# Load order and router weights in a one-core language-model tower: seven loads held behind the first gathers, one expert weight ahead of the first tile rows, router weights made during the expert tiles

## The chip, the core and the metric

The kernel runs on one core of a Trainium2 chip. The metric is the device time of one execution in microseconds (us). The kernel before was timed three times: median 885.13 us, from 883.92 to 888.87.

## What is computed

Token ids (32 sequences of 96) go through three residual blocks; everything is in 32-bit floating point.

```python
x = emb[tokens] * sqrt(128) + positional
q, k, v = x @ Wq + bq, x @ Wk + bk, x @ Wv + bv
scores = einsum('d,bijd->bij', attn_scale, tanh(q[:, :, None, :] + k[:, None, :, :]))
x = layer_norm(x + softmax(scores) @ v @ Wo + bo)
h = layer_norm(x + relu(x @ W1 + bf1) @ W2 + bf2)
h = h + causal_attention_8_heads(layernorm(h))
...
n = layernorm_affine(layernorm(h))
vals, idx = top_2(softmax(n @ Wr @ codebook.T / 0.7))
w = vals / sum(vals)
moe = sum over the two chosen of 64 experts of w * (silu(n @ W1[e] + b1[e]) @ W2[e] + b2[e])
hmoe = moe + 0.25 * (silu(n @ Ws1 + bs1) @ Ws2 + bs2)
return h + hmoe + silu(layernorm_affine(hmoe) @ Wf1 + fbf1) @ Wf2 + fbf2
```

Since the two weights of a token sum to one, they follow from the gap between its second and first logit: with g = exp(gap / 0.7) they are 1 / (1 + g) and g / (1 + g).

## The kernel before

The program is written engine by engine. Each engine runs its own list in order, and semaphores tie them together. SP issues nearly all loads, GpSimd (POOL) the indirect ones.

**Start.** SP sends the ids, then five small loads (semaphore `ld_a`), then seven loads under `ld_b` (wvT, wo, and the five of `ROWS`, each one row of 512 bytes repeated over 128 partitions). VectorE makes indices from the ids, and GpSimd gathers the embedding rows of the first two pairs of sequences with four indirect loads (semaphores `emb0` and `emb1`, 16 * G for a pair, line 491). SP waits for `emb0` and then sends 15 `late` loads, of which the first four are 512 KB each. With `emb0` there, VectorE's `x_rows(0)` (line 904) starts the work. `setup` on TensorE (lines 1343 and 1344), between the first two blocks of scores, and on VectorE (lines 913 to 915) wait for all of `ld_b`. `products` (line 1366) waits for all of `late`.

**Pairs.** 16 pairs of sequences go through a software pipeline (`in_turns`), in which each engine has a fixed order of stages of up to six pairs. Beside it SP fills a region of DRAM with zeros (`rows_dram`, 64 experts with room for every token) and stores x. At the end of a pair each token's row is scattered twice into `rows_dram`, to the next free place of each of its two experts.

**Expert tiles.** From the counts VectorE builds a table of tiles of 128 rows (`ttab`): some 84 tiles, of which 52 (`FIXED`) are written out and the rest run in loops of 8. For each tile SP loads the weights of its expert (`load_expert`, 578 KB, 16 slots) and the rows are loaded (`load_rows`, 64.5 KB, 8 buffers; the first 8 by SP, the others by ScalarE). TensorE transposes rows (line 1635), multiplies with the first weight (1642), ScalarE applies SiLU (771), TensorE multiplies with the second (1653), VectorE adds the bias (1216), and GpSimd stores the results with an indirect store (`store_rows`, 590). The order in which SP starts is set by `ROWS_FIRST`:

```python
for t in range(ROWS_FIRST):
    load_expert(t)
sp.wait_ge(s["scat"], 16 * TOPK * B)
load_rows(sp, 0)
for t in range(1, ROWS_AHEAD):
    load_rows(sp, t)
    load_expert(t + ROWS_FIRST - 1)
```

After weight 23 (slot reuse waits for the tile 16 before) SP loads the residual back from DRAM (`x_back`, 3072 rows of 512 bytes) and then goes on with weight 24. VectorE waits in `hb_affine(t)` (line 1210) until the store of tile t - 8 has landed. The gaps of the logits are brought into token order by TensorE at tile 9 (`relay`) and copied by VectorE at tile 11 (`take_relaid`, semaphore `gaps_t`).

**Last stage.** The shared expert is computed for 12 blocks of 256 tokens: eight of them before the tiles, the last four (`SHARED_LATE`) behind them (TensorE 1525 and 1535, ScalarE 706, VectorE's `shared_rows`, 1092). SP loads the results back block by block (`er0` and on). ScalarE makes exp(gap / 0.7) with an exchange of its table before and after (lines 792 to 794); VectorE makes the two weights (1256 to 1260) and then, for each block, `mixture` (1267 to 1286, with a power on GpSimd, 603, for the square root) and `output` (1295); TensorE has `f_turn` (1689), `last1` (1697) and `last2` (1708).

## Time and profile before

| | us |
|---|---|
| median of three runs | 885.13 |
| lowest and highest | 883.92, 888.87 |
| the profiled execution | 880.4 |
| its span in the profile | 878.6 |

| engine | busy us (share of the span) |
|---|---|
| TensorE (PE) | 781.5 (89%) |
| TensorE weight loads (PEld) | 603.4 (69%) |
| VectorE (DVE) | 656.6 (75%) |
| ScalarE (ACT) | 657.5 (75%) |
| GpSimd (POOL) | 323.0 (37%) |

The profile page gives busy times, the DMA queues and the chain that ended last; the trace behind it gives each instruction's start and duration, what ended the idle time before it, the granted clock of TensorE (1.00 is 2.4 GHz, 0.50 is 1.2 GHz) and the busy share of the 16 DMA engines in any stretch. All times below count from the start of the span. An `SPq` row is a DMA issue by SP; of a row that stands for several instructions (x4), the second number is their time together.

### The profile page before, as it was taken

Reading aid. Unit: us, or ns where it says so; the run is one execution under the profiler, and the core shown is the slowest. Engines: PE = TensorE matmul, PEld = TensorE weight load, DVE = VectorE, ACT = ScalarE, POOL = GpSimd, SP = SyncE. Lnnn points to the kernel's source line nnn. Section 1 sums busy time; section 2 is a strip of 40 time slices with the busy share of each in tenths; the row PEclk is TensorE's granted clock in tenths of the full one; section 3 lists DMA queues with packets and bytes.
Section 4 is the critical chain, followed back from the end, with each engine's and each line's share of the span. In section 5 each row is a group of like instructions: output and inputs, shape, how many; then the busy total and the mean of one; then the engine's idle time right before and its main releaser. Section 6 shows DMA issues by size and latency. Waiting matters only on the chain. (4 is left out here: it accounts for less than half of the span.)

```text
span 878.6 us, 22649 instructions
## 1 busy us (share of the span) xinstructions
PE 781.5 (89%) x7286; PEld 603.4 (69%) x7286; DVE 656.6 (75%) x2161; ACT 657.5 (75%) x1502; POOL 323.0 (37%) x397
## 2 busy tenths in 40 slices
PE   1777998988998989989899999898889999999798
PEld 0454675665665766756667666665679999999687
DVE  3999889989999999999999999453523435443675
ACT  2787989989898898988998999675335655655454
POOL 3110322325334343353343432444414545545121
PEclk9999999999999999999999999997989999999799
DMA  7239889889889889989898898894199999994411
GB/s 149 65 83 210 190 188 210 194 189 212 186 196 210 187 198 207 197 189 206 181 211 181 182 209 178 195 208 97 45 321 397 377 395 403 307 362 161 150 30 37
DMA packets 82305, 177.77 MB, mean 202 GB/s; under 512 B 8244, under 2 KB 35339, under 8 KB 82240
## 3 DMA queue, kind: packets, MB, share of 16 engines
q1 hardware_dynamic: 65536, 164.01, 74.8%
q0 software_dynamic: 5760, 7.92, 2.7%
q10 hardware_dynamic: 10944, 5.02, 2.1%
q8 instruction: 35, 0.57, 0.3%
q14 instruction: 30, 0.25, 0.1%
HBM read 65.93 MB, written 113.34 MB: 204 GB/s over the span
## 5 line engine op out<-in xcount | busy, mean ns | idle before, releaser
L890 DVE TENSOR_TENSOR arena<-qT,b_qk 128x2304 f32<-128x2304 f32 x128 | 323.8, 2543 | 1.6 <-DVE v_bias L915 0.3
L616 ACT ACTIVATE arena<-arena 128x2304 f32<-128x2304 f32 x128 | 271.6, 2123 | 35.7 <-DVE arena L890 34.4
L1322 PE MATMUL b_s<-arena,apad 128*32 128x192 f32 x3072 | 159.2, 343 | 27.1 <-ACT p L625 18.5
L771 ACT ACTIVATE act_h<-big,arena 128x128 f32<-128x128 f32 x336 | 95.8, 368 | 74.6 <-PE big L1642 70.2
L1322 PEld LDWEIGHTS b_s<-arena,apad 128*32 128x32 f32 x3072 | 89.9, 113 | 83.9 <-issue 41.5
L542 POOL TENSOR_TENSOR kept<-kept,rs 96x384 f32<-96x384 f32 x64 | 52.6, 823 | 208.2 <-DVE rs L1025 208.0
L590 POOL DMA_INDIRECT eo_dram<-gT,toff x84 | 82.5, 982 | 97.2 <-issue 67.1
L668 ACT ACTIVATE kept<-kept,mx 96x96 f32<-96x96 f32 x256 | 92.3, 365 | 13.3 <-DVE mx L1018 13.3
L1642 PE MATMUL big<-hbT,arena 128*128 128x128 f32 x672 | 91.1, 279 | 2.4 <-DVE hbT L1205 1.4
L1642 PEld LDWEIGHTS big<-hbT,arena 128*128 128x128 f32 x672 | 83.4, 195 | 3.2 <-issue 2.3
L1205 DVE TENSOR_SCALAR hbT<-b_t,cols 128x128 f32<-128x128 f32 x84 | 34.4, 409 | 65.4 <-PE b_t L1635 65.4
L1489 PEld LDWEIGHTS b_o<-vv,prT 96*96 96x96 f32 x512 | 61.0, 165 | 13.2 <-issue 10.8
L1489 PE MATMUL b_o<-vv,prT 96*96 96x128 f32 x512 | 68.6, 278 | 0.0
L560 POOL DMA_INDIRECT rows_dram<-rows_now,slot_now x64 | 61.1, 955 | 17.8 <-issue 15.6
L1449 PE MATMUL big<-kept,xaT 128*96 128x512 f32 x128 | 66.1, 600 | 0.0
L1018 DVE CUSTOM_DVE_ANT_0 kept<-big,mask 96x96 f32<-96x96 f32 x256 | 49.2, 249 | 18.9 <-PE big L1464 15.7
L1464 PE MATMUL big<-gT,xaT 128*96 128x384 f32 x128 | 54.0, 505 | 2.5 <-DVE mx L1018 2.5
L668 ACT ACTIVATION_READ_ACCUMULATOR kept<-kept,mx 96x1 f32 x256 | 49.1, 192 | 0.0
L1439 PE MATMUL big<-xaT,kept 128*128 128x192 f32 x256 | 46.7, 326 | 0.4 <-ACT xaT L653 0.4
L662 ACT ACTIVATE vv<-big 96x512 f32<-96x512 f32 x64 | 38.0, 594 | 10.1 <-PE big L1449 9.8
L1653 PE MATMUL b_s<-arena,act_h 128*128 128x128 f32 x336 | 45.1, 278 | 0.0
L1653 PE MATMUL b_qk<-arena,act_h 128*128 128x128 f32 x336 | 44.5, 275 | 0.3 <-ACT act_h L771 0.3
(208 smaller groups left out, 1413.8 us busy)
## 6 DMA issues: line engine op xcount, KB each, us to landing
rows_dram<-act_h SPq DMA_DIRECT2D x32, 3096.0 KB
arena<-in_wpack SPq DMA_DIRECT2D x84, 578.0 KB
prT<-rows_dram ACTq DMA_DIRECT2D x76, 64.5 KB
arena<-eo_dram SPq DMA_DIRECT2D x4, 512.0 KB, 7.2
x_dram<-res SPq DMA_DIRECT2D x16, 96.0 KB
out<-of SPq DMA_DIRECT2D x12, 128.0 KB, 1.8
eo_dram<-gT,toff POOLq DMA_INDIRECT x84
rows_dram<-rows_now,slot_now POOLq DMA_INDIRECT x64
```

Source lines behind the costliest of these rows:

```text
L560: pool.indirect_dma_start(rows_dram, bass.IndirectOffsetOnAxis(ap=slot_now[:, j:j + 1].bitcast(U32), axis=0), rows_now[:, j, :], None, bou ...
L590: pool.indirect_dma_start(eo_dram, bass.IndirectOffsetOnAxis(ap=toff[:, r:r + 1].bitcast(U32), axis=0), eo[r], None, bounds_check=TOPK * T ...
L616: act.activation(v, v, ACT.Tanh).then_inc(s["tanh"], 1)
L668: last = act.activation(pr[:, j, :], pr[:, j, :], ACT.Exp, bias=mx2[:, j:j + 1], scale=-1.0, accum_out=es2[:, j:j + 1])
L771: last = act.activation(act_h[:, i, c * TILE:(c + 1) * TILE], big[i][:, c * TILE:(c + 1) * TILE], ACT.Silu, bias=wslot[:, slot, 2 * DFF + ...
L890: dve.tensor_tensor(ring[c % TRING].rearrange("p (x m n) -> p x m n", m=CQ, n=N), qv.unsqueeze(3).to_broadcast([D, SPLIT * QG, CQ, N]), kv ...
L1322: last = pe.matmul(b_s[32 * a:32 * a + 32, 0:SPLIT * N], apad[:, 31 - line:63 - line], t[:, :, a, m, :], start=(line == 0), stop=(line == ...
L1449: pe.matmul(BANK_V[k][0:N, :], xaT[:, g * N:(g + 1) * N], vo[:, (k % 2) * 512:(k % 2 + 1) * 512], start=True, stop=True).then_inc(s["hv"], 1)
L1464: pe.matmul(BANK_S[k][0:N, 0:4 * N], xaT[:, g * N:(g + 1) * N], gT[:, h:h + 4, g * N:(g + 1) * N], start=True, stop=True).then_inc(s["s2"], 1)
L1489: last = pe.matmul(p_o[:, g, :], prT[:, g * H + h, :], vv[:, g, h * D:(h + 1) * D], start=False, stop=(k == 3 and h == H - 1))
L1642: last = pe.matmul(big[of_ring(t, 2)][:, c * TILE:(c + 1) * TILE], wslot[:, slot, c * D:(c + 1) * D], hbT[:, of_ring(t, 2), :], start=True ...
L1653: last = pe.matmul([b_s, b_qk][of_ring(t, 2)][:, 0:D], act_h[:, of_ring(t, 2), c * TILE:(c + 1) * TILE], wslot[:, slot, DFF + c * D:DFF + ...
```

## The change

Three things change.

1. SP's wait for `emb0` stands ahead of the seven `ld_b` loads, which now follow it, with the 15 late ones behind.
2. `ROWS_FIRST` is 1, not 3: SP sends one weight, rows 0, rows 1, weight 1, rows 2, weight 2 and so on. From the 18th of these loads on the order is the same.
3. exp(gap / 0.7) is made on GpSimd as a power of the constant exp(1 / 0.7) (`weigh`, after the store of tile 12), and the two weights on VectorE in tiles 21, 22 and 23. ScalarE's Exp and its two exchanges of tables at the end are gone. Two of the four late shared blocks (`shared_rows` 10 and 11) move behind the residual sum of `mixture(0)`, and TensorE's wait for them from before `f_turn(0)` into `last2(0)`.

```diff
--- before.py
+++ after.py
@@ -43,7 +43,7 @@
 NO_ID = 8192
 SHARED_LATE = 4
 RESIDUALS = 3
-ROWS_FIRST = 3
+ROWS_FIRST = 1
 QG = 4
 SPLIT = 2
 QM = N // (QG * SPLIT)
@@ -174,6 +174,7 @@
         gaps = sb("gaps", [N, PAIRS * G])
         gaps_t = sb("gaps_t", [128, NT])
         gap_e = sb("gap_e", [128, NT])
+        base_e = sb("base_e", [128, NT])
         wts = sb("wts", [128, NT, TOPK])
         rows_now = sb("rows_now", [N, G * TOPK, DC])
         slot_now = sb("slot_now", [N, G * TOPK], I32)
@@ -372,12 +373,12 @@
             load(wqk[:, 1, :], io["L0_tok_Wk"], s["ld_a"])
             load(cols[:, :], io["cols"], s["ld_a"])
 
+            sp.wait_ge(s["emb0"], 16 * G)
             load(wvT[:, :], io["tok_WvT"], s["ld_b"])
             load(wo[:, :], io["L0_tok_Wo"], s["ld_b"])
             for n in ROWS:
                 load(rows[n][:, :], io["row_" + n].partition_broadcast(128), s["ld_b"])
 
-            sp.wait_ge(s["emb0"], 16 * G)
             for i, n in enumerate(["Wq", "Wk", "Wv", "WoT"]):
                 load(raw[:, i, :].rearrange("p (h d) -> p h d", h=H),
                      io["attn_" + n].rearrange("(h k) d -> k h d", h=H), s["late"])
@@ -498,6 +499,7 @@
                     b = p * G + g
                     gather_rows(res[0:N, p, g, :], eidx[:, b:b + 1], s[f"emb{p}"])
             pool.memset(halves[:, 2 * G:], 0.5)
+            pool.memset(base_e[:, :], float(np.exp(1.0 / TEMP)))
             pool.memset(fhalf[:, :], -0.5).then_inc(s["pool_c"], 1)
             pool.memset(cum, 0.0).then_inc(s["pool_c"], 1)
             pool.iota(choice[:, :], [[TOPK * N, B], [1, TOPK]], base=-NO_ID, channel_multiplier=TOPK,
@@ -591,8 +593,14 @@
                     eo_dram, bass.IndirectOffsetOnAxis(ap=toff[:, r:r + 1].bitcast(U32), axis=0),
                     eo[r], None, bounds_check=TOPK * T - 1, oob_is_err=False).then_inc(s_st[r], 16)
 
+            def weigh():
+                pool.wait_ge(s["gaps_t"], 1)
+                pool.tensor_tensor(gap_e[:, :], base_e[:, :], gaps_t[:, :], ALU.pow).then_inc(s["gap_e"], 1)
+
             for t in range(FIXED):
                 store_rows(t)
+                if t == RELAY + 3:
+                    weigh()
             blocks = blocks_less(pool, 0)
             with pool.Fori(0, blocks) as v:
                 for r in range(BLOCK):
@@ -787,11 +795,6 @@
             for j in range(NB - SHARED_LATE, NB):
                 silu_shared(j)
 
-
-            act.wait_ge(s["gaps_t"], 1)
-            act.preload_act_table(ACT.Exp)
-            act.activation(gap_e[:, :], gaps_t[:, :], ACT.Exp, scale=1.0 / TEMP).then_inc(s["gap_e"], 1)
-            act.preload_act_table(ACT.Silu)
 
             def silu_last(j):
                 for c in range(FC):
@@ -1222,6 +1225,17 @@
                                 b_y[:, NT * TOPK:NT * (TOPK + 1)].rearrange("p (a m) -> p a m", a=TILES3))\
                     .then_inc(s["gaps_t"], 1)
 
+            def weights(i):
+                if i == 0:
+                    dve.wait_ge(s["gap_e"], 1)
+                    ch.link(dve.tensor_scalar(gaps_t[:, :], gap_e[:, :], 1.0, None, ALU.add))
+                elif i == 1:
+                    ch.wait()
+                    ch.link(dve.reciprocal(wts[:, :, 0], gaps_t[:, :]))
+                else:
+                    ch.wait()
+                    ch.link(dve.tensor_tensor(wts[:, :, 1], gap_e[:, :], wts[:, :, 0], ALU.mult))
+
             def add_fbf2(i):
                 if i == 0:
                     dve.wait_ge(s["x_back"], 16)
@@ -1235,6 +1249,8 @@
                     eo_copy(t - 2)
                 if t == RELAY + 2:
                     take_relaid()
+                if RELAY + 12 <= t < RELAY + 15:
+                    weights(t - RELAY - 12)
                 if FIXED - 4 <= t < FIXED:
                     add_fbf2(t - FIXED + 4)
             blocks = blocks_less(dve, 0)
@@ -1250,15 +1266,8 @@
             eo_copy((last, BLOCK - 1))
 
 
-            for j in range(NB - SHARED_LATE, NB):
+            for j in range(NB - SHARED_LATE, NB - 2):
                 shared_rows(j)
-            dve.wait_ge(s["gap_e"], 1)
-            ch.link(dve.tensor_scalar(gaps_t[:, :], gap_e[:, :], 1.0, None, ALU.add))
-            ch.wait()
-            ch.link(dve.reciprocal(wts[:, :, 0], gaps_t[:, :]))
-            ch.wait()
-            ch.link(dve.tensor_tensor(wts[:, :, 1], gap_e[:, :], wts[:, :, 0], ALU.mult))
-            ch.wait()
 
             def mixture(j):
                 dve.wait_ge(s[f"er{result_sem(j)}"], 16)
@@ -1279,6 +1288,9 @@
                 dve.tensor_scalar(fve[:, :], fmv[:, :, 1], EPS, None, ALU.add).then_inc(s["fve"], 1)
                 ch.link(dve.tensor_tensor(rh[j % RESIDUALS], hm[:, :, :], xr[:, j, :].rearrange("p (g d) -> p g d", g=G),
                                           ALU.add))
+                if j == 0:
+                    for i in range(NB - 2, NB):
+                        shared_rows(i)
                 dve.wait_ge(s["frstd"], j + 1)
                 if j:
                     dve.wait_ge(s["fT_ps"], j)
@@ -1700,7 +1712,9 @@
                         last.then_inc(s["f1"], 1)
 
             def last2(j):
-                if not (known(j) and j == 0):
+                if known(j) and j == 0:
+                    pe.wait_ge(s["ysh"], NB)
+                else:
                     pe.wait_ge(s["of"], j)
                 for c in range(FC):
                     pe.wait_ge(s["fa"], FC * j + c + 1)
@@ -1716,7 +1730,6 @@
                 shared1(j)
                 shared2(j - 1)
             shared2(NB - 1)
-            pe.wait_ge(s["ysh"], NB)
             f_turn(0)
 
             def step(j):
```

On SP, at the start, before (`cols` is the last of `ld_a`, `wvT` the first and `row_fbf` the last of `ld_b`, `arena<-in_attn_Wq` the first late load):

```order
L365 DMA cols<-in_cols 128x21
L365 DMA wvT<-in_tok_WvT 128x128
L365 DMA wo<-in_L_tok_Wo 128x128
...
L365 DMA row_fbf<-in_row_fbf 128x128
L365 DMA arena<-in_attn_Wq 128x8x128 [waits s_emb0]
```

And now:

```order
L366 DMA cols<-in_cols 128x21
L366 DMA wvT<-in_tok_WvT 128x128 [waits s_emb0]
L366 DMA wo<-in_L_tok_Wo 128x128
...
L366 DMA row_fbf<-in_row_fbf 128x128
L366 DMA arena<-in_attn_Wq 128x8x128
```

The order is the same, and the wait has moved up by seven loads.

On SP, where the tiles begin, before (`arena<-in_wpack` is an expert's weight, `prT<-rows_dram` the rows of a tile):

```order
L429 DMA arena<-in_wpack 128x1156
...
L429 DMA arena<-in_wpack 128x1156
...
L429 DMA arena<-in_wpack 128x1156
L349 TENSOR_LOAD ttab [waits s_scat]
...
L350 DMA prT<-rows_dram 128x129
...
L350 DMA prT<-rows_dram 128x129
...
L429 DMA arena<-in_wpack 128x1156
```

And now:

```order
L430 DMA arena<-in_wpack 128x1156
L350 TENSOR_LOAD ttab [waits s_scat]
...
L351 DMA prT<-rows_dram 128x129
...
L351 DMA prT<-rows_dram 128x129
...
L430 DMA arena<-in_wpack 128x1156
```

The first two rows loads have moved up past two weights, which now come later.

On VectorE, behind the last tile, before (`kept<-b_s,bs2q` is a shared block, `gaps_t` and `wts` are the weights, `vv<-arena,wts,kept` begins the first mixture, `gT<-hm,fmv,frstd` is its normalised end):

```order
L1092 SCALAR_TENSOR_TENSOR kept<-b_s,bs2q 128x256 [waits s_ys]
L1092 SCALAR_TENSOR_TENSOR kept<-b_qk,bs2q 128x256 [waits s_ys]
L1092 SCALAR_TENSOR_TENSOR kept<-b_s,bs2q 128x256 [waits s_ys]
L1092 SCALAR_TENSOR_TENSOR kept<-b_qk,bs2q 128x256 [waits s_ys]
L1256 TENSOR_SCALAR gaps_t<-gap_e 128x24 [waits s_gap_e]
L1258 RECIPROCAL wts<-gaps_t 128x24 [waits s_chain]
L1260 TENSOR_TENSOR wts<-gap_e,wts 128x24 [waits s_chain]
L1267 SCALAR_TENSOR_TENSOR vv<-arena,wts,kept 128x128 [waits s_er0,s_chain]
...
L1280 TENSOR_TENSOR vv<-hm,res 128x256
L1286 TENSOR_SCALAR gT<-hm,fmv,frstd 128x128 [waits s_frstd]
```

And now:

```order
L1095 SCALAR_TENSOR_TENSOR kept<-b_s,bs2q 128x256 [waits s_ys]
L1095 SCALAR_TENSOR_TENSOR kept<-b_qk,bs2q 128x256 [waits s_ys]
L1276 SCALAR_TENSOR_TENSOR vv<-arena,wts,kept 128x128 [waits s_er0]
...
L1289 TENSOR_TENSOR vv<-hm,res 128x256
L1095 SCALAR_TENSOR_TENSOR kept<-b_s,bs2q 128x256 [waits s_ys]
L1095 SCALAR_TENSOR_TENSOR kept<-b_qk,bs2q 128x256 [waits s_ys]
L1298 TENSOR_SCALAR gT<-hm,fmv,frstd 128x128 [waits s_frstd]
```

The three instructions for the weights have gone to the tiles, and two shared blocks stand within the first mixture.

## Rows read from the trace of the kernel before

**Rows 1.** Timeline, start: start us, us, engine, line, operation, operands, count [idle before <- what ended it].
```profile
3.55 0.43 SPq L365 DMA_DIRECT2D wvT<-in_tok_WvT  x1
...
5.86 0.97 POOL L491 DMA_INDIRECT res<-in_L_tok_emb,eidx  x1 [0.31 <-issue]
...
12.51 0.42 DVE L904 SCALAR_TENSOR_TENSOR xs<-res,pe_rows 96x256 f32<-96x256 f32 x1 [7.10 <-DMA res<-in_L_tok_emb,eidx]
...
23.19 0.80 PE L1343 MATMUL big<-wo,wvT 128*128 128x128 f32 x2
...
35.52 0.96 POOL L491 DMA_INDIRECT emb<-in_L_tok_emb,eidx_now  x1 [0.31 <-issue]
```

**Rows 2.** Timeline of TensorE in the tiles, products of tiles 23 and 24.
```profile
690.99 1.06 PE L1642 MATMUL big<-hbT,arena 128*128 128x128 f32 x8
...
692.89 1.06 PE L1642 MATMUL big<-hbT,arena 128*128 128x128 f32 x8
```

**Rows 3.** Stretches: length, busy (instructions) PE PEld DVE ACT POOL, granted clock, DMA share, GB/s.
```profile
643.00:649.00 6.00, 5.10 (x22) 4.73 (x23) 0.99 (x5) 1.86 (x7) 0.00 (x0) 0.50 0.96 301
...
685.00:690.00 5.00, 5.00 (x48) 5.00 (x47) 1.90 (x9) 2.92 (x11) 2.60 (x3) 1.00 1.06 352
...
824.00:830.00 6.00, 5.42 (x17) 4.57 (x18) 4.59 (x20) 2.65 (x6) 1.49 (x2) 0.50 0.02 8
```

**Rows 4.** Timeline at the end of the tiles, all engines.
```profile
815.13 0.42 DVE L1092 SCALAR_TENSOR_TENSOR kept<-b_qk,bs2q 128x256 f32<-128x256 f32 x1 [1.33 <-PE b_qk L1535]
...
816.89 1.16 PE L1535 MATMUL b_qk<-ws,act_h 128*128 128x128 f32 x8
...
819.18 0.61 DVE L1267 SCALAR_TENSOR_TENSOR vv<-arena,wts,kept 128x128 f32<-128x128 f32 x2
...
823.26 0.66 PE L1689 MATMUL b_o<-ident,gT 128*128 128x128 f32 x2 [5.22 <-DVE gT L1286]
```

**Rows 5.** DMA from 0 to 40 us, 40 slices of 1 us: busy tenths; GB/s.
```profile
DMA  0035335958771269999999999920000000002100
GB/s 0 9 98 140 76 96 36 28 27 96 113 146 59 52 177 346 298 289 290 291 291 331 309 277 306 328 57 0 0 16 0 0 0 0 0 12 37 49 0 0
```

**Rows 6.** Timeline of TensorE, first use of the late loads.
```profile
41.81 3.08 PE L1366 MATMUL big<-arena 128*128 128x128 f32 x24
```

**Rows 7.** Timeline of SP's DMA issues (SPq) around the first tiles.
```profile
634.29 2.63 SPq L429 DMA_DIRECT2D arena<-in_wpack  x3
637.69 1.42 SPq L350 DMA_DIRECT2D prT<-rows_dram  x2
...
652.96 16.20 SPq L429 DMA_DIRECT2D arena<-in_wpack  x15
```

**Rows 8.** Timeline of TensorE, first transpose, products of tiles 0 and 2.
```profile
642.21 0.33 PE L1635 MATMUL b_t<-ident,prT 128*128 128x128 f32 x1 [2.90 <-DMA prT<-rows_dram]
...
643.40 2.05 PE L1642 MATMUL big<-hbT,arena 128*128 128x128 f32 x8 [0.86 <-DVE hbT L1205]
...
649.84 1.06 PE L1642 MATMUL big<-hbT,arena 128*128 128x128 f32 x8
```

**Rows 9.** Timeline of SP's DMA issues: weight 24.
```profile
671.03 14.30 SPq L429 DMA_DIRECT2D arena<-in_wpack  x1
```

**Rows 10.** DMA issues: out<-in, engine, operation, count, KB, us from issue to landing.
```profile
arena<-in_attn_Wq SPq DMA_DIRECT2D x1, 512.0 KB, 4.1
...
arena<-in_attn_WoT SPq DMA_DIRECT2D x1, 512.0 KB, 7.1
...
arena<-eo_dram SPq DMA_DIRECT2D x1, 256.0 KB, 2.8
```

**Rows 11.** GpSimd's powers: duration in ns (least/median/most), first and last start, forms.
```profile
L537 POOL TENSOR_TENSOR rstd_h<-ve_h,halves x16: 1318/1361/1363, 129.5 to 616.8; 96x6 f32<-96x6 f32 x16
...
L603 POOL TENSOR_TENSOR frstd<-fve,fhalf x12: 798/800/922, 821.6 to 868.0; 128x2 f32<-128x2 f32 x12
```

**Rows 12.** Timeline of GpSimd in the tiles: result store 13.
```profile
677.09 0.98 POOL L590 DMA_INDIRECT eo_dram<-gT,toff  x1 [0.92 <-issue]
```

## The prediction

> **What bounds the kernel now.** I read the share of each engine by stage, then the timeline at the three places that the change touches, then the waits there. From 30 to 600 us VectorE, ScalarE and TensorE work through 16 pairs of sequences in one fixed order, so a start that comes earlier moves the whole stage. The start is one chain: the second gather of embedding rows is issued at 5.86, VectorE waits 7.10 us for it and begins at 12.51, and everything else hangs on that [rows 1]. In the expert tiles (640 to 810 us) TensorE is full, one tile per 1.90 us [rows 2], while the DMA share is over 1.0 [rows 3]: two resources are close to their limit at once. The last stage is one chain on VectorE, and TensorE stands still for 5.2 us ahead of it [rows 4].
>
> **The loads behind the gathers.** Removed: seven loads that stood ahead of the gathers' packets. Before, the gather needed 12.51 - 5.86 = 6.65 us. From 7 to 8 us (eighth digit of the view in 1 us slices) the DMA engines are shown fully busy and move 28 GB/s [rows 5]: the five row loads that repeat one row over 128 partitions keep them busy with next to nothing. The same gather with no load beside it is issued at 35.52 [rows 1], and its bytes have passed by 38, the last slice with traffic (49 GB/s, then 0) [rows 5]: 2.4 us. So the first rows land near 5.86 + 2.4 = 8.3 and the chain gains 12.5 - 8.3 = **4.2 us**. Bounds: 0 (all of the 6.65 us is the gather's own) and 4.5.
>
> Added: SP waits for the gathers with the seven loads and the 15 late ones queued behind. They took from 3.55 [rows 1] to at most 12.5, where SP sends the first late load: 9 us, so now 8.3 + 9 = 17.3. TensorE asks for them at 23.19 - 4.2 = 19.0 [rows 1]: 1.7 us of cover, and should it be gone, TensorE's queue, with the scores behind it, waits by as much. The late loads are through by 27 [rows 5], now by some 31, and are wanted at 41.81 - 4.2 = 37.6 [rows 6]: nothing.
>
> **One weight ahead of the first rows.** SP issues one load per 1.09 us. Before: three weights from 634.29, rows 0 at 637.69 [rows 7]. Now rows 0 go out at 634.29 + 1.09 = 635.4 with one weight ahead of them instead of three, and are there when TensorE is free at 639.3 (it then idled 2.90 us and made the first transpose at 642.21 [rows 8]). From transpose to first expert product took 1.2 us, so tile 0 starts at 640.5, not 643.40: 2.9 us. Since that idle stretch goes, so does the half clock after it (0.50 from 643 to 649 [rows 3]): two tiles took 649.84 - 643.40 = 6.4 us [rows 8] instead of 3.8, another 2.6. Against it: rows and weights come one pair per 2.18 us until tile 8, slower than 1.90, which takes back about 1.0. TensorE is then 4.5 us ahead.
>
> It can't keep that. From the 18th load on, SP's list is the same load at the same time: 15 weights from 652.96, back to back [rows 7], then the load of the residual in 3072 short rows, and weight 24 whose issue is held for 14.30 us, from 671.03 to 685.33 [rows 9]. Loads of similar size landed 4.1 to 7.1 us after their issue [rows 10], so weight 24 is there between 689.4 and 692.4; I take 691.4, towards the late end, as the DMA share stands at 1.06 [rows 3]. TensorE used it at 692.89 [rows 2]. The slack is 1.5 us (0.5 to 3.5), and rows and results of two tiles more will have passed by then, some 0.5 us. So tile 24 starts **1.0 us** earlier, not 4.5, and TensorE stands about 3.5 us before it. That stop has a price: the clock was 0.50 after the idle stretches of 2.9 and of 5.2 us [rows 3]. At 0.50 a tile takes up to twice as long, and here nothing absorbs it: between 0 and 5 us; I take 2.0, a little under the 2.6 above. The whole edit: 1.0 us slower. Bounds: 3.0 faster (slack 3.5, no half clock), 4.5 slower.
>
> **Router weights in the tiles.** Removed from the end: Exp with two table loads on ScalarE, three VectorE instructions. VectorE waits little for Exp, but the three and the last two shared blocks stand ahead of the first mixture at 819.18 [rows 4]. Now it follows the second shared block (815.13 + 0.42 = 815.6 [rows 4]) and the first results, issued at 813.05, which landed 2.8 us later, at 815.9 [rows 10]. So it starts at 815.9: 3.3 us earlier. The two shared blocks moved behind its residual sum cost 0.8 us, of which 0.6 lies in VectorE's wait for GpSimd's root; their products are ready at 818.05 [rows 4], and VectorE comes to them at about 818.6. Left: **3.0 us** for the first normalised block, at TensorE 820.3 instead of 823.26 [rows 4]. Bounds 2.6 and 3.6; the upper if TensorE, idle 2.2 us instead of 5.2, keeps its clock and VectorE never waits for it.
>
> Added: a power of 128x24 on GpSimd between result stores 12 and 13, and three short VectorE instructions in tiles 21 to 23. The power on 6 columns takes 1.36 us and on 2 columns 0.80 [rows 11], 0.14 us per column, so 24 columns take 0.8 + 22 x 0.14 = 3.9 us (0.8 to 8). A store takes 0.98 and has 0.92 idle ahead of it [rows 12]; the next one is late by 3 us and each turn catches up 0.6. VectorE needs a store landed eight tiles on, and a small excess falls into TensorE's wait at tile 24. Cost: nothing. The three VectorE instructions take 0.7 us (the gap between the last shared block and the mixture), in tiles in which VectorE works 1.90 of 5 us [rows 3]. The new memset lies beside the gathers' flight.
>
> **Sum:** -4.2 + 1.0 - 3.0 = -6.2 us, against the profiled execution 880.4 -> 874.2. That execution was 4.7 below the median, so I carry the difference: 885.1 - 6.2 = **878.9 us**. A measurement tells about 0.5% (4.4 us) from no change.
>
> **Rivals.**
> 1. *No stop, or no half clock, at tile 24.* Weight 24 lands early, or TensorE's wait stays under what lowers the clock. For: the held issue of 14.30 us may shrink. Against: a DMA share of 1.06 right there. The second edit then gains 1.0 to 3.0: 885.1 - 8.2 = 876.9 with the first, 875 with the second.
> 2. *The gather's time is its own.* The first gathers are the first work of their queue, and the first edit gains nothing. Against it: the one at 35.52 took 2.4 us with the same number of rows. Sum: 885.1 - 2.0 = 883.1. The Trainium skill (DMA: Bandwidth & Descriptors, Queues, rings and completion order) says that a DMA engine takes turns between the queues it has work for, packet by packet; by that rule loads in another queue would hold the gather back by a few packets only, and this rival's 883.1 would be the time.
> 3. *Slower: GpSimd's power.* Its base varies from that of the powers in the trace. GpSimd stands still for X us; VectorE's wait for store 13, or for the power itself in tile 21, then blocks the transposed rows, and TensorE with them. About 8 us of X are covered (some 4 before VectorE needs it, 3.5 in the stop at tile 24), then each costs one. To be slower by 4.4 us over all, X must be over 8 + 7.2 + 4.4 = 20 us; at 25 us, 885.1 - 7.2 + 17 = 895. Every power in the trace is under 1.4 us, so this is unlikely.
> 4. *The seven loads are late for the set-up*, at 19.0: each us over costs one. If they take 3 us longer than before, 1.3 us are lost: 880.2.
>
> **How the numbers follow.** Forecast 0.45; rival 1 0.27; rival 2 0.15; rival 3 0.04; rival 4 and single low clocks elsewhere 0.09. Range: from 873.5 (rival 1 with the upper bounds of both other gains) to 883.5 (rival 2). Faster by over 0.5% (under 880.7): rival 1, four fifths of the forecast (the rest for one more stretch of low clock, 2 to 5 us) and a third of rival 4: 0.67. Slower: 0.05. Within 0.5%: 0.28.
>
> **What would show it.** The first VectorE row on the embeddings near 8.3; TensorE's set-up without a wait; tile 0 near 640.5 less 4.2; one idle stretch of about 3.5 us at TensorE before tile 24, with a granted clock of 0.50 right behind; the power at 3.9 us; the first mixture 2.8 us after the first result load's issue, and no table load on ScalarE there. I am wrong on the first edit if the gather still takes over 5 us, on the second if the tiles run through without a stop or if it is elsewhere, on the third if the mixture starts over 1 us after its results.

## The result, and the profile after

The changed kernel takes **877.5 us** (median of 18 runs, 870.9 to 883.8) against 884.2 of the kernel before beside it: a ratio of 0.9924, 95% interval 0.9898 to 0.9949, or 6.7 us less (4.5 to 9.0). The forecast was -6.2 us and 878.9 us. Its profiled execution lasted 881.04 us (span 879.2), one of its longer ones, while that of before was one of its shorter ones (880.4). So the two traces are compared stage by stage, not by their ends.

The start, in the timeline of the changed kernel (same columns as [rows 1]; lines have moved by 1 to 12):

```profile
6.00 0.97 POOL L492 DMA_INDIRECT res<-in_L_tok_emb,eidx  x1 [0.31 <-issue]
...
8.93 0.33 SPq L366 DMA_DIRECT2D wvT<-in_tok_WvT  x1
8.94 0.42 DVE L907 SCALAR_TENSOR_TENSOR xs<-res,pe_rows 96x256 f32<-96x256 f32 x1 [3.40 <-DMA res<-in_L_tok_emb,eidx]
...
11.67 0.43 SPq L366 DMA_DIRECT2D row_fbf<-in_row_fbf  x1
...
19.62 0.50 PEld L1355 LDWEIGHTS big<-wo,wvT 128*128 128x128 f32 x2 [0.60 <-DMA row_fbf<-in_row_fbf]
19.62 0.80 PE L1355 MATMUL big<-wo,wvT 128*128 128x128 f32 x2
```

The gather is through in 8.94 - 6.00 = 2.94 us instead of 6.65, and VectorE begins 3.57 us earlier. The seven loads took from 8.93 until just before 19.6 (the last is issued at 11.67 and lands 7.9 us later by the list of DMA issues shown at the end), 10.6 us and not 9: the weight load of the set-up names that last one as what ended its idle time, but the product starts exactly 3.57 us earlier than in [rows 1]. The 1.7 us of cover that I counted were at most 0.1.

The DMA engines over the same 40 us, in slices of 1 us ([rows 5]):

```profile
DMA  0034202111562012269999999998559321000000
GB/s 0 10 108 119 32 0 43 28 43 50 144 70 29 11 51 65 56 201 282 328 246 299 246 263 333 315 285 234 145 153 304 92 43 34 22 0 0 16 0 0
```

The slices from 7 to 10 us now show little work (1 tenth each) where 9, 5 and 8 stood. The row loads themselves, which land between 14.2 and 19.6 us here, do not fill the engines either: the slices from 12 to 17 show 2, 0, 1, 2 and 2 tenths. The late loads end at about 31 us, and TensorE takes them at 38.17, again 3.6 earlier than in [rows 6].

The turn to the tiles. First VectorE's copy of the router table of before, which is what the tile loads wait for, then the same of the changed kernel:

```profile
632.47 0.39 DVE L1197 CAST ttab<-b_y 1x234 int32<-1x234 f32 x1 [1.85 <-PE b_y L1611]
```

```profile
635.20 0.39 DVE L1200 CAST ttab<-b_y 1x234 int32<-1x234 f32 x1 [1.12 <-PE b_y L1623]
```

So in this execution the lead of 3.6 us has become a lag of 2.7. The granted clock is the likeliest reason; the stretches from 13 to 600 and from 600 to 640 us, of before and of after (columns as [rows 3]):

```profile
13.00:600.00 587.00, 524.19 (x5303) 363.11 (x5304) 526.94 (x1610) 510.97 (x1040) 206.47 (x262) 0.98 0.87 188
600.00:640.00 40.00, 33.40 (x184) 26.27 (x183) 17.14 (x103) 17.67 (x54) 17.55 (x21) 0.83 0.22 62
```

```profile
13.00:600.00 587.00, 524.07 (x5296) 362.04 (x5296) 525.88 (x1601) 510.35 (x1038) 206.03 (x261) 0.97 0.89 189
600.00:640.00 40.00, 34.16 (x170) 26.93 (x171) 17.04 (x111) 17.09 (x53) 18.40 (x22) 0.74 0.14 38
```

In the last stretch the clock was 0.74 against 0.83: more time at 1.2 GHz. How much of the 6.3 us this explains was not worked out. Such stretches fall elsewhere in every execution (for the same code the table stands at 635.20 here and at 632.99 in e9), so the stage that follows is measured from the router table.

The first tiles ([rows 8]); each row is the first product of a tile:

```profile
643.08 1.13 PE L1654 MATMUL big<-hbT,arena 128*128 128x128 f32 x8 [0.93 <-DVE hbT L1208]
644.82 1.16 PE L1654 MATMUL big<-hbT,arena 128*128 128x128 f32 x8 [0.51 <-DVE hbT L1208]
647.15 1.13 PE L1654 MATMUL big<-hbT,arena 128*128 128x128 f32 x8 [0.17 <-DMA arena<-in_wpack]
649.60 1.13 PE L1654 MATMUL big<-hbT,arena 128*128 128x128 f32 x8 [0.32 <-DMA arena<-in_wpack]
653.07 1.13 PE L1654 MATMUL big<-hbT,arena 128*128 128x128 f32 x8 [1.34 <-DMA arena<-in_wpack]
```

Tile 0 starts 643.08 - 635.20 = 7.9 us behind the table instead of 643.40 - 632.47 = 10.9, and at full clock (1.13 us for eight products, not 2.05). But TensorE then waits for weights at tiles 2, 3 and 4. The one of tile 4 is used at 653.07, 6.1 us after SP issued it:

```profile
646.96 0.33 SPq L430 DMA_DIRECT2D arena<-in_wpack  x1
```

SP's issues and TensorE around weight 24 ([rows 9], [rows 2]), and the power with the stores behind it ([rows 11], [rows 12]):

```profile
674.52 16.11 SPq L430 DMA_DIRECT2D arena<-in_wpack  x1
...
696.75 1.13 PE L1654 MATMUL big<-hbT,arena 128*128 128x128 f32 x8 [1.42 <-DMA arena<-in_wpack]
```

```profile
676.74 4.21 POOL L598 TENSOR_TENSOR gap_e<-base_e,gaps_t 128x24 f32<-128x24 f32 x1
681.14 1.03 POOL L592 DMA_INDIRECT eo_dram<-gT,toff  x1 [0.19 <-issue]
682.47 0.98 POOL L592 DMA_INDIRECT eo_dram<-gT,toff  x1 [0.30 <-issue]
683.75 0.97 POOL L592 DMA_INDIRECT eo_dram<-gT,toff  x1 [0.30 <-issue]
685.03 0.97 POOL L592 DMA_INDIRECT eo_dram<-gT,toff  x1 [0.30 <-issue]
687.87 0.97 POOL L592 DMA_INDIRECT eo_dram<-gT,toff  x1 [1.87 <-DVE gT L1219]
```

The issue of weight 24 is held again, 16.11 us instead of 14.30, and TensorE waits for it at 696.75: in the place foretold, shorter than foretold, with no half clock behind it (the eight products take 1.13 us). The power takes 4.21 us (forecast 3.9), and four stores follow it back to back. And there is a stop that I had not foreseen, in VectorE's sums of results (gT) right then:

```profile
682.27 0.29 DVE L1219 TENSOR_TENSOR gT<-b_s,arena 128x128 f32<-128x128 f32 x1 [0.42 <-issue]
...
686.81 0.29 DVE L1219 TENSOR_TENSOR gT<-b_qk,arena 128x128 f32<-128x128 f32 x1 [2.37 <-PE b_s L1665]
```

Tile 17's sum comes 4.54 us behind tile 16's; 1.90 is the rule. VectorE is shown waiting for TensorE's products, whose rows for this tile end at 684.1.

The end of the tiles ([rows 4]):

```profile
817.79 5.21 SPq L366 DMA_DIRECT2D arena<-eo_dram  x8
...
819.09 0.42 DVE L1095 SCALAR_TENSOR_TENSOR kept<-b_qk,bs2q 128x256 f32<-128x256 f32 x1 [1.33 <-PE b_qk L1547]
...
820.52 0.61 DVE L1276 SCALAR_TENSOR_TENSOR vv<-arena,wts,kept 128x128 f32<-128x128 f32 x2 [1.01 <-DMA arena<-eo_dram]
...
824.51 0.69 PE L1701 MATMUL b_o<-ident,gT 128*128 128x128 f32 x2 [2.50 <-DVE gT L1298]
```

The mixture starts 820.52 - 817.79 = 2.7 us after the first result load's issue, as forecast (2.8). TensorE stands for 2.50 us, not 5.22. No table load stands on ScalarE here.

### The profile page after: what moved, and what is told of

The parts are those of the page before. It is cut to its first block and busy times, and to the rows that moved or that the text cites. A ratio compares the mean times of both kernels' runs of the same rounds, so it can differ in the third digit from the quotient of the medians.

```text
span 879.2 us, 22647 instructions
## 1 busy us (share of the span) xinstructions
PE 785.0 (89%) x7286; PEld 603.5 (69%) x7286; DVE 656.3 (75%) x2161; ACT 654.7 (74%) x1499; POOL 327.1 (37%) x399
## 5 line engine op out<-in xcount | busy, mean ns | idle before, releaser
L1208 DVE TENSOR_SCALAR hbT<-b_t,cols 128x128 f32<-128x128 f32 x84 | 34.4, 409 | 65.6 <-PE b_t L1647 60.5
L1021 DVE CUSTOM_DVE_ANT_0 kept<-big,mask 96x96 f32<-96x96 f32 x256 | 49.2, 249 | 21.8 <-PE big L1476 19.1
L534 POOL TENSOR_TENSOR rstd_x<-ve_x,halves 96x2 f32<-96x2 f32 x32 | 23.2, 724 | 58.7 <-DVE ve_x L951 58.2
## 6 DMA issues: line engine op xcount, KB each, us to landing
prT<-rows_dram ACTq DMA_DIRECT2D x76, 64.5 KB
```

## The experiments

Where each execution was, from the router table on, in us: VectorE's sum of results of tile n less the start of the table's copy; then, from the sum of tile 83 on, the first mixture and the output sums of the last block (the first of the two).

| kernel | tile 0 | 8 | 16 | 24 | 83 | mixture | last sum |
|---|---|---|---|---|---|---|---|
| before | 17.6 | 32.7 | 49.2 | 64.4 | 177.2 | 9.5 | 65.9 |
| changed | 11.8 | 30.6 | 47.1 | 65.6 | 178.5 | 6.9 | 62.6 |
| e1 | 17.8 | 33.6 | 50.1 | 65.2 | 176.7 | 9.5 | 65.3 |
| e2 | 11.8 | 29.9 | 46.4 | 68.2 | 179.7 | 9.5 | 65.6 |
| e3 | 17.6 | 33.5 | 50.0 | 65.2 | 176.7 | 6.1 | 61.6 |
| e4 | 17.6 | 33.5 | 50.0 | 65.2 | 176.7 | 6.2 | 61.8 |
| e5 | 11.8 | 30.6 | 47.1 | 64.2 | 177.7 | 6.1 | 61.6 |
| e6 | 17.1 | 32.7 | 49.2 | 67.9 | 181.5 | 6.2 | 62.3 |
| e7 | 18.1 | 34.1 | 50.6 | 65.8 | 178.7 | 9.5 | 65.1 |
| e8 | 17.4 | 33.2 | 49.7 | 64.9 | 177.8 | 9.5 | 65.1 |
| e9 | 11.8 | 29.6 | 46.1 | 64.4 | 179.6 | 6.2 | 61.8 |
| e10 | 11.8 | 29.7 | 46.2 | 61.6 | 176.0 | 6.1 | 61.7 |
| e11 | 18.2 | 34.2 | 50.7 | 66.0 | 180.8 | 6.1 | 61.7 |
| e12 | 18.0 | 33.2 | 49.7 | 68.1 | 183.3 | 8.7 | 64.5 |

Theory: the gather was choked by the loads; the head start in the tiles is given back at weight 24; the router weights at the end are pure gain. Rivals: the start is absorbed later; the power disturbs the tiles; the DMA engines are simply full.

**e1, the first edit alone.**

```
+            sp.wait_ge(s["emb0"], 16 * G)
             load(wvT[:, :], io["tok_WvT"], s["ld_b"])
             load(wo[:, :], io["L0_tok_Wo"], s["ld_b"])
             for n in ROWS:
                 load(rows[n][:, :], io["row_" + n].partition_broadcast(128), s["ld_b"])
-            sp.wait_ge(s["emb0"], 16 * G)
```

> The kernel before with the seven loads held behind the first gathers, and nothing else. Theory 'loads choke the gather': VectorE's first work on the embeddings starts near 8.9 us instead of 12.51, TensorE's set-up at 19.6 shows no wait on the loads, and the kernel is 3.6 us faster (879 to 881). Rival 'the start is absorbed later' (the pair stage is held by something that does not move): first work at 8.9 but the router table is ready less than 1.5 us earlier than before, and the time gains under 1.5 us.

Measured: 878.0 against 882.7, ratio 0.9956 (0.9937 to 0.9976), 3.9 us less (2.1 to 5.6). The first work is at 8.77 instead of 12.51, and the set-up follows at 19.44 instead of 23.19, as much earlier:

```profile
8.77 0.42 DVE L904 SCALAR_TENSOR_TENSOR xs<-res,pe_rows 96x256 f32<-96x256 f32 x1 [3.34 <-DMA res<-in_L_tok_emb,eidx]
...
19.44 0.80 PE L1343 MATMUL big<-wo,wvT 128*128 128x128 f32 x2
```

The timed gain is that of the start, as far as the interval can tell (2.1 to 5.6), and the rival's under 1.5 us is out. In the trace the router table stands at 629.96 instead of 632.47, 2.5 us earlier; with clocks that differ between executions, this pair does not say whether the missing 1.2 us were absorbed.

**e2, the second edit alone.**

```
-ROWS_FIRST = 3
+ROWS_FIRST = 1
```

> The kernel before with one weight ahead of the first tile rows, and nothing else. Theory 'weight 24 sets it': tile 0 starts 3 us earlier behind the router table, no half clock follows, by tile 8 about 2 us of the 5.7 are left, TensorE waits 2 to 4 us for weight 24, and from there on the tiles are 0 to 1.5 us later behind the table than before: 884.5 to 886. Rival 'the power ate it': without the power on GpSimd there is no stop at tiles 17 to 19, weight 24 comes in time, and the kernel is 1.5 to 3 us faster.

Measured: 883.7 against 882.7, ratio 1.0007 (0.9990 to 1.0024): no difference, where the forecast had 1.0 us slower. The stop of the forecast is here in full, on TensorE, and the clock behind it (the stretch in the columns of [rows 3]):

```profile
690.69 1.06 PE L1642 MATMUL big<-hbT,arena 128*128 128x128 f32 x8
696.59 2.05 PE L1642 MATMUL big<-hbT,arena 128*128 128x128 f32 x8 [3.85 <-DMA arena<-in_wpack]
700.36 1.81 PE L1642 MATMUL big<-hbT,arena 128*128 128x128 f32 x8
703.00 1.06 PE L1642 MATMUL big<-hbT,arena 128*128 128x128 f32 x8
```

```profile
695.00:702.00 7.00, 5.41 (x26) 5.44 (x26) 0.76 (x3) 1.14 (x4) 0.34 (x1) 0.51 1.03 409
```

Tile 24 comes 5.90 us behind tile 23, 4.0 over the rule (forecast 3.5), and the next two take 6.41 us instead of 3.79: 2.6 for the half clock (forecast 2.0). The table of the router stands at 634.98, so weight 24 was used 61.6 us behind it, against 692.89 - 632.47 = 60.4 before. I had it 1.0 us earlier; it is 1.2 later. There is no gap at tiles 17 to 19, so the expectation's rival is out. At tile 83 this execution is 2.5 us behind before and 3.0 behind e1; the timed runs allow at most 2.1, so it shows more of a loss than the median of the runs has, and why is open.

**e3, the third edit alone.** Against the changed kernel:

```
-ROWS_FIRST = 1
+ROWS_FIRST = 3
...
-            sp.wait_ge(s["emb0"], 16 * G)
             load(wvT[:, :], io["tok_WvT"], s["ld_b"])
...
+            sp.wait_ge(s["emb0"], 16 * G)
             for i, n in enumerate(["Wq", "Wk", "Wv", "WoT"]):
```

> The kernel before with the router weights made during the tiles and two shared blocks moved behind the first mixture, and nothing else. Theory 'hidden': the power of 128x24 takes 4.2 us, no tile starts later for it, the first mixture starts 6.9 us instead of 9.5 us after the last result sum, and the kernel is 2.6 to 3.0 us faster. Rival 'the power delays the stores and the tiles with them': tiles 17 to 19 come 1.5 to 2 us late as in the changed kernel, nothing takes that back, and only 1 us is gained.

Measured: 878.5 against 882.7, ratio 0.9940 (0.9916 to 0.9963), 5.3 us less (3.3 to 7.4), more than forecast (3.0). In its table row the tiles are those of e1, with the power of 4.21 us and six stores back to back: hidden, as forecast. The end gains 65.3 - 61.6 = 3.7 us against e1, 4.3 against before: the mixture is 3.4 us earlier, and 0.3 us lie behind it. The clock stays at full there (see e4), but e5, with some 3.4 us at 0.50 in that place, has the same 61.6, so the 0.3 us can't be put down to the clock.

**e4, the changed kernel with three weights ahead.**

```
-ROWS_FIRST = 1
+ROWS_FIRST = 3
```

> The changed kernel with three weights ahead of the first tile rows, as before. If the edit of the weights costs 1.0 us, as forecast, this is 1.0 us faster than the changed kernel: 7.6 us faster than before. If that edit gains (the stop at weight 24 is smaller than its head start), this is 4 to 6 us faster than before, and slower than the changed kernel.

Measured: 876.1, ratio 0.9926 (0.9900 to 0.9952), 6.5 us less than before; the changed kernel had 6.7. The second edit is worth nothing that can be told, in either direction. And e4 has just the edits of e1 and e3, whose gains would make 9.2 us together: beside e1's 3.9 us the third edit brings 2.6 more here, not the 5.3 that it measured alone; each of the three ratios is known to some 2 us only, so both can be noise about one value. The forecast's 3.0 and the 3.7 of the traces lie between the two. TensorE ahead of the first normalised block, and the stretch from there on:

```profile
819.55 0.44 PE L1701 MATMUL b_o<-ident,gT 128*128 128x128 f32 x2 [1.84 <-DVE gT L1298]
```

```profile
819.50:826.00 6.50, 5.07 (x31) 4.22 (x32) 5.33 (x22) 2.81 (x6) 1.12 (x2) 1.00 0.73 243
```

With 1.84 us of idleness no half clock follows here, where it did beside 2.50 and 5.22. That the shorter idleness is the reason is not shown: in e5, e6, e9 and e10 the clock fell beside 1.72 to 1.86 us (last section). The router tables of e3 and e4 also answer the question of the start: both executions had a granted clock of 0.97 from 13 to 600 us and of 0.87 from 600 to 640, the first work on the embeddings was at 12.95 and 8.66, and the tables came at 636.13 and 632.67. Of 4.3 us at the start 3.5 arrive at the table.

**e5, the changed kernel with the residual's load 16 tiles later.**

```
-                if t == BLOCK:
+                if t == 3 * BLOCK:
```

> The changed kernel with the load of the residual (3072 short rows) 16 tiles later on SP, behind weight 39 instead of weight 23. Theory 'the held issue of weight 24': weight 24 is issued and landed in time, TensorE's wait of 1.4 us (5.9 us in the kernel with one weight alone) before tile 24 is gone, the head start of 3 us at tile 8 is kept, and the kernel is 2.5 to 4 us faster than the changed kernel: a ratio to before of 0.988 to 0.990. Weight 40 is held then; it has some 9 us of slack. Rival 'the DMA engines are full': the wait moves to a neighbouring tile or to rows and the kernel gains under 1 us.

Measured: 878.7 against 885.6, ratio 0.9912 (0.9884 to 0.9939). The changed kernel had 0.9924, so the 2.5 to 4 us are not there. Tile 24 did come 1.4 us earlier behind the table (64.2), but behind the stop at tile 17 (4.7 us from sum to sum) smaller gaps (2.6 to 2.8 us) stand at tiles 19, 21, 23, 25 and 28, and by tile 83 0.8 us are left. The held issue moved to weight 40 (14.85 us) and no wait for a weight stands there. The rival's time came out (some 1 us), but not its reason: the rows of these gaps name TensorE's products and no load, so that the DMA engines are full is not shown. (The 5.9 us that the expectation gives for e2 are from product to product; TensorE's wait was 3.85.)

**e6, the same with three weights ahead.** The edit is e4's and e5's together.

> The same with three weights ahead of the first tile rows. There was no wait at tile 24 in it, so both theories expect no change against the changed kernel with three weights: 0.9926. If the DMA traffic as such slows the tiles, up to 1 us is gained here too.

Measured: 881.9 against 885.6, ratio 0.9955 (0.9929 to 0.9982). No gain from the later load, as both said; the intervals of e4 and e6 overlap. Its trace has the same stop behind the power as the changed kernel's, which e4 did not have. By tile 24 it is 2.7 us behind e4 (67.9 against 65.2). VectorE's sums of tiles 16 and 17, in e4 and in e6:

```profile
682.71 0.29 DVE L1219 TENSOR_TENSOR gT<-b_s,arena 128x128 f32<-128x128 f32 x1 [0.42 <-PE b_s L1665]
684.61 0.29 DVE L1219 TENSOR_TENSOR gT<-b_qk,arena 128x128 f32<-128x128 f32 x1 [0.42 <-PE b_qk L1665]
```

```profile
682.02 0.29 DVE L1219 TENSOR_TENSOR gT<-b_s,arena 128x128 f32<-128x128 f32 x1 [0.42 <-issue]
686.63 0.29 DVE L1219 TENSOR_TENSOR gT<-b_qk,arena 128x128 f32<-128x128 f32 x1 [1.70 <-remote]
```

**e7 and e8, which loads choke the gather.** In e7 only the five row loads are held and the two weight loads stay ahead; in e8 only the two are held.

The diff of e7 (in e8 the first two loads and the loop change places around the wait):

```
             load(wvT[:, :], io["tok_WvT"], s["ld_b"])
             load(wo[:, :], io["L0_tok_Wo"], s["ld_b"])
+            sp.wait_ge(s["emb0"], 16 * G)
             for n in ROWS:
                 load(rows[n][:, :], io["row_" + n].partition_broadcast(128), s["ld_b"])
-            sp.wait_ge(s["emb0"], 16 * G)
```

> The kernel before with only the five repeated-row loads held behind the first gathers; the two weight loads of 64 KB stay ahead. Theory 'the repeated rows choke the gather': VectorE's first work on the embeddings at 8.8 to 9.3 us. Rival 'any load behind the gathers does it': in proportion to bytes (5 of 7 loads held), some 9.9 us.

> The kernel before with only the two weight loads held; the five repeated-row loads go out ahead, 0.9 us earlier than before. Theory 'the repeated rows choke the gather': first work on the embeddings at 11.5 to 12.5 us, no gain worth the name. Rival 'any load does it': some 11.4 us.

Measured, one execution each. The timeline of e7, then that of e8:

```profile
5.78 0.97 POOL L491 DMA_INDIRECT res<-in_L_tok_emb,eidx  x1 [0.31 <-issue]
...
8.75 0.42 DVE L904 SCALAR_TENSOR_TENSOR xs<-res,pe_rows 96x256 f32<-96x256 f32 x1 [3.23 <-DMA res<-in_L_tok_emb,eidx]
```

```profile
5.88 0.97 POOL L491 DMA_INDIRECT res<-in_L_tok_emb,eidx  x1 [0.31 <-issue]
...
11.43 0.42 DVE L904 SCALAR_TENSOR_TENSOR xs<-res,pe_rows 96x256 f32<-96x256 f32 x1 [6.02 <-DMA res<-in_L_tok_emb,eidx]
```

From issue to first use: 2.97 us with the two weight loads ahead of the gather, 5.55 with the five rows, 6.65 with all seven [rows 1], 2.94 with none (e1 and the changed kernel). The two plain loads of 64 KB cost 0.0; the repeated rows cost 2.6 alone and 3.7 with the two loads ahead of them. It is e7 that decides: the rival "any load, by bytes" had 9.9 for it and 8.75 was measured, while e8's 11.43 is also what the rival had (11.4). One more difference stays: in e7 the two plain loads are issued at 3.55 and 4.03 and land 1.9 and 2.1 us later, so they are all but through when the gather is issued at 5.78; the row loads are not. Five plain loads in the rows' place were not tried. What is shown is that the row loads, still under way beside the gather, are what delays it. How they do it is open: in e7, from 11 to 16 us, where only they and the start of the late loads behind them are under way, the DMA engines are busy by shares of 0.10 to 0.23.

**e9, the changed kernel again**, to see whether the stop behind the power comes back.

> The changed kernel once more, beside the three below. Its first profile had a stop of about 2 us at tiles 17 to 19, behind the power, when GpSimd sent four delayed stores one every 1.28 us. Theory 'the backlog of stores stops the tiles': the stop stands here again. Rival 'a chance event': no gap over 2.1 us at tiles 16 to 20, and TensorE's wait at tile 24 is longer by the same 2 us (3 to 4 us).

Measured: 879.6 against 886.1, ratio 0.9921 (0.9890 to 0.9952). The stop is there again: 4.72 us from the sum of tile 16 to that of tile 17, and TensorE waits 0.97 us at tile 24. The single chance event is out: the stop comes back in the same kernel.

**e10, the power in four pieces** (on top of e5).

A piece follows stores 12, 16, 20 and 24:

```
-                pool.tensor_tensor(gap_e[:, :], base_e[:, :], gaps_t[:, :], ALU.pow).then_inc(s["gap_e"], 1)
+                cut = slice(i * NT // 4, (i + 1) * NT // 4)
+                pool.tensor_tensor(gap_e[:, cut], base_e[:, cut], gaps_t[:, cut], ALU.pow).then_inc(s["gap_e"], 1)
...
-                if t == RELAY + 3:
-                    weigh()
+                if RELAY + 3 <= t < RELAY + 19 and (t - RELAY - 3) % 4 == 0:
+                    weigh((t - RELAY - 3) // 4)
...
-                if RELAY + 12 <= t < RELAY + 15:
-                    weights(t - RELAY - 12)
+                if RELAY + 24 <= t < RELAY + 27:
+                    weights(t - RELAY - 24)
```

> The changed kernel with the residual's load 16 tiles later, and the power cut into four of 128x6, one behind every fourth store from store 12 on; the weights are made in tiles 33 to 35. A piece should take about 1.36 us, as the power on 96x6 did, so that a store is late by 0.5 to 1 us and no backlog of three stores forms. Theory 'the backlog of stores stops the tiles': the stops at tiles 17 to 28 that stood in the kernel with the later load go, and tile 83 comes 1.5 to 3 us earlier behind the router table (175 to 176 us instead of 177.7); the best of the series at 0.988 to 0.990 of before. Rival 'a full DMA': the gaps stay and the time is that of the kernel with the later load, 0.991.

Measured: 878.8 against 886.1, ratio 0.9914 (0.9885 to 0.9943). A piece takes 1.35 to 1.37 us and the latest store is late by some 0.7 us, as expected. Tile 83 came 176.0 us behind the table, 1.7 earlier than in e5, but the single stop has become gaps of 2.6 to 3.0 us at tiles 15, 17, 19, 27, 29 and 32, and the time is that of e5. Neither theory is borne out cleanly.

**e11, the same pieces with three weights ahead.**

> The changed kernel with three weights ahead and the power in four pieces. If the backlog costs the tiles something, this is 0.5 to 2 us faster than the whole power with three weights (0.9926 of before); if the power was hidden, as forecast, there is no difference beyond 0.25%.

Measured: 880.5, ratio 0.9943 (0.9921 to 0.9965), within the intervals of e4 and e6. The trace has gaps of 2.7 to 3.1 us at seven tiles between 15 and 32, so a shorter backlog did not remove them.

**e12, the two shared blocks back ahead of the mixture** (on top of e4).

```
-            for j in range(NB - SHARED_LATE, NB - 2):
+            for j in range(NB - SHARED_LATE, NB):
                 shared_rows(j)
...
-                if j == 0:
-                    for i in range(NB - 2, NB):
-                        shared_rows(i)
```

> The changed kernel with three weights ahead, and the last two shared blocks put back ahead of the first mixture. Their products are there 8.3 us after the last result sum, so the first mixture starts 8.7 to 9 us after it instead of 6.1, and the kernel loses 2.0 to 2.8 us against the one with three weights. Rival: only the three VectorE instructions and the Exp held the mixture, it starts at 7 us, and less than 1 us is lost.

Measured: 886.2 against 886.1, ratio 0.9998 (0.9972 to 1.0024). That is 6.4 us lost against e4's ratio, where 2.0 to 2.8 was expected; the sign was right, the size too small. The stretch of the end is 64.5 instead of 61.8 us: the first mixture comes at 8.7 instead of 6.2, right behind the last shared block,

```profile
825.00 0.42 DVE L1095 SCALAR_TENSOR_TENSOR kept<-b_qk,bs2q 128x256 f32<-128x256 f32 x1 [0.77 <-PE b_qk L1544]
825.34 0.60 DVE L1276 SCALAR_TENSOR_TENSOR vv<-arena,wts,kept 128x128 f32<-128x128 f32 x2
...
829.41 0.66 PE L1698 MATMUL b_o<-ident,gT 128*128 128x128 f32 x2 [4.44 <-DVE gT L1295]
```

and beside TensorE's 4.44 us of idleness the granted clock is 0.50 again. TensorE's wait for these two blocks also stands ahead of its first turn again, as before. That makes 2.8 us. The measured loss is larger (0.72% against e4, 0.55% against e11, 0.43% against e6, which has the same power and the stop behind it), and e12's own tiles were slow (183.3, against 181.5 in e6 and 176.7 in e4); what the rest is due to was not settled.

**No version beats the changed kernel** by more than the measurement can tell: e5 0.9912, e10 0.9914, e9 0.9921, the changed kernel 0.9924, e4 0.9926.

## Why the prediction was right, point by point

- **The loads behind the gathers: right in what delays the gather, not shown in how.** Forecast 4.2 us, measured 3.9 (2.1 to 5.6) by e1, 3.6 in the trace. The gather took 2.94 us, not 2.4, and its issue was 0.14 later. That the row loads hold the gather back is confirmed by e7 and e8. That they do it by keeping the DMA engines busy with next to nothing was read from one digit and one GB/s figure of [rows 5], where the gather was under way too; by themselves the same loads show 0 to 2 tenths (changed kernel, 12 to 17 us) and are slow all the same. Rival 2, the gather's own time, would have been 883.1: the gather's 2.94 us reject it. The Trainium skill (DMA: Bandwidth & Descriptors, Queues, rings and completion order) has a DMA engine take turns between queues packet by packet. No run here shows the order of the packets. That this would cost the gather a few packets only was my inference, and it is wrong for the repeated rows: the gather waited 2.6 us on them. The two plain loads do not test it, since they were nearly through before the gather.
- **The seven loads for the set-up: right, by luck.** Forecast cover 1.7 us, measured at most 0.1. The loads took 10.6 us from the first issue, not 9; they begin and are wanted with the gather, so its being 0.6 us later than I had it changed little. Rival 4 was one small step away.
- **The head start in the tiles: the mechanism right, three terms mis-sized.** Tile 0 gained 3.0 us behind the router table (forecast 2.9), and the half clock went (2.7, forecast 2.6). What the feeding takes back until tile 8 was forecast as 1.0 us by the issue rate alone; it is 3.6 in the changed kernel and 3.0 in e2. The weights landed late, and TensorE waited for the DMA, not for SP (tile 4's weight was used 6.1 us after its issue). Weight 24 was not 1.0 earlier but 1.2 later behind the table. The stop it makes was 4.0 and the half clock 2.6 in e2. The net was +1.0 in the forecast; the traces say +2.5 for e2 and +1.2 for the changed kernel, and the timed runs 0.6 slower (0.9 faster to 2.1 slower) for e2. Of what I said would show it, the place is right; the length (1.42 us) and the half clock are wrong for the changed kernel. The stop at tile 17 comes before it and can have taken a part of it, since in e2, without that stop, the wait was 3.85; and that stop is itself one "elsewhere", which I had named as a sign of being wrong. In this it looked like rival 1, but for another reason.
- **Router weights in the tiles: right.** Forecast 3.0 us. e3 measured 5.3 alone (3.3 to 7.4), e4 less e1 gives 2.6; the traces say 3.7 to 4.3 for e3 and 3.3 for the changed kernel. So the size is known to a microsecond or two only, and the forecast is inside that or a little low. The mixture came 2.7 us behind its results' issue in the changed kernel, as said, and 3.4 us earlier in e3 than in e1 (forecast 3.3). I had taken 3.0 between bounds of 2.6 and 3.6; the traces of e3 and e4 come out at the upper bound (TensorE's first turn is 3.5 and 3.4 us earlier behind the last tile). The larger part of it is the two shared blocks moved behind the residual sum, which the forecast counted without a price of its own: without it the first mixture is 2.5 us later (e12).
- **The power: the size right, the cost open.** Forecast 3.9 us and hidden, measured 4.21. In e3 and e4 it is hidden to the last tenth of a microsecond. In the changed kernel, e5, e6, e9 and e12 3.2 to 4.7 us from sum to sum stand at tile 17, beside the four stores that follow the power back to back. In no execution without the power is there one there (before, e1, e2, e7, e8). So it comes with the power, but not always (e3 and e4 have six stores back to back and no stop); and a shorter power, in pieces, spread the gaps rather than removing them. e1 to e4 ran on one chip, e5 to e8 on a second and e9 to e12 on a third, at other times, and a small gap at tile 39, at which GpSimd sends three late stores back to back in every version, shows the same division: none in e1 to e4, 3.2 to 3.6 us from sum to sum in all others. Why that is so, and whether executions without the profiler stop there too, stays open. It is rival 3 in the small: 1.3 to 2.8 us over the rule at tile 17 in these traces, and not 17.
- **The sum.** By the runs of single edits: -3.9, +0.6 and -5.3, together -8.6 us. The changed kernel has -6.7, within the intervals. The forecast's -6.2 is close partly by luck: the second edit's +1.0 lies within the timed interval although two of its terms were off by 2.2 and 2.6 us, and the stop behind the power was not in the sum. The lower end of the range, 873.5, is half a microsecond below what its parts give (885.1 - 4.5 - 3.0 - 3.6 = 874.0), and the upper end, 883.5, is 0.4 above rival 2's 883.1; nothing hangs on either.

## What to carry to other kernels

A load that is needed later can still be what delays the first gather: look at how long each load takes to land for its bytes, and hold the slow ones (here the repeated rows) behind it. A head start into a stage whose loads are close to the limit of the DMA engines is given back inside the stage (here all of 5.7 us), so count what has to land by the first stop, not when the first item starts. And where one short chain restarts an idle engine, take everything off it that can run beside it: the place of two small blocks moved the end by 2.8 us in the traces here.

## What the runs showed of the hardware that I had not expected

- Loads that repeat one row over 128 partitions land slowly even where the DMA engines are little used (2, 0, 1, 2 and 2 tenths from 12 to 17 us): in the changed kernel's list of DMA issues (columns of [rows 10]), all of 64 KB,

```profile
wvT<-in_tok_WvT SPq DMA_DIRECT2D x1, 64.0 KB, 2.0
...
row_bo<-in_row_bo SPq DMA_DIRECT2D x1, 64.0 KB, 4.4
...
row_fbf<-in_row_fbf SPq DMA_DIRECT2D x1, 64.0 KB, 7.9
```

- The time that the granted clock stood at 0.50 beside TensorE's idleness ahead of the first normalised block did not follow the length of that idleness. Beside 5.21 and 5.22 us it was about 10.2 us (before, e2) or 6.8 (e1, e7, e8); beside 4.44 (e12) and 2.50 (changed) about 6.8; beside 1.83 (e6) also about 6.8, beside 1.72 (e5, e10) and 1.86 (e9) about 3.4, and beside 1.71 (e3), 1.75 (e11) and 1.84 (e4) it did not fall at all. So a shorter idleness gives a better chance of full clock here, and no more.
- The issue that SP holds behind the load of 3072 short rows took 14.3 us before and 16.1 in the changed kernel, and 12.9 to 15.0 in the others that have it at weight 24; at weight 40 it took 14.9 (e5), 11.0 (e6) and 17.2 (e10). Putting the load later did not make it reliably shorter.
